# Gates and decoders of the experts: operands as two float32r parts with three products, and a second layer with early decay rates and one batch normalised by VectorE

## The reference, cut to what matters

```python
# one expert e; B = 4 batches of S = 512 tokens, D = 256 hidden features, 128 model features
mem = jnp.concatenate([hf, hb], axis=-1)                       # 512 features
gate_s = jax.nn.sigmoid(jax.nn.relu(mem @ sw1 + sb1) @ sw2 + sb2)
gate_t = jnp.tanh(jax.nn.relu(mem @ tw1 + tb1) @ tw2 + tb2)
g = gate_s * gate_t
out_e = _ln(jax.nn.relu(g @ dw1 + db1) @ dw2 + db2, dg, dbeta) # summed over e with the router's weights
...
# second layer: x = layer norm of the sum h
dt = sigmoid(x @ dt_w + dt_b) * 0.099 + 0.001
dA = exp(dt * -exp(A_log));  dBu = dt * (x @ B_mat.T)
hs[t] = dA[t] * hs[t - 1] + dBu[t]                             # over the 512 tokens of a batch
h = h + layer_norm(hs @ C_mat.T + D_vec * x) * gamma + beta
z = layer_norm(h)
out = h + (gelu(z @ tril(W1).T + b1) @ tril(W2).T + b2)        # over 128 features
```

## Time and profile before

| | |
|---|---|
| time, median of 3 runs | 5180.55 us (5178.99 to 5180.73) |
| the profiled execution: its own time | 5181.15 us |
| its span, first to last instruction | 5179.3 us |
| TensorE busy in the span | 5021.1 us, 97% |
| mean granted clock | 0.985 |
| the 16 steps on TensorE | 4695.4 us to about 5111 us |
| the second layer behind them | about 5111 us to 5179.3 us |

### The profile page before, as it was taken

How to read it: one execution, slowest core, us unless ns; L and a number is a source line. 1 busy time by engine, 2 the same in 40 slices (tenths; PEclk the granted TensorE clock), 3 DMA queues, 4 the chain that set the end, 5 groups by cost and what they waited for, 6 DMA issues and landing times. The chain is left out here.

```text
span 5179.3 us, 257985 instructions
## 1 busy us (share of the span) xinstructions
PE 5021.1 (97%) x108736; PEld 3531.4 (68%) x108736; DVE 4071.9 (79%) x19244; ACT 2374.2 (46%) x8355; POOL 1272.9 (25%) x5271
## 2 busy tenths in 40 slices
PE   7989799999999999999999999999999999998997
PEld 4656333333333337999999999999999999994444
DVE  3857666666666657999999999999999999992225
ACT  2734465555555543444444444444444444442334
POOL 0000032222221112333333333333333333330000
PEclk9989899999999999999999999999999999999998
DMA  0024644645544442110111011101111011102120
GB/s 15 1 89 155 144 100 120 137 119 127 122 114 106 97 167 91 25 41 17 41 25 41 17 41 25 41 21 37 41 25 41 18 41 25 41 1 91 50 69 10
DMA packets 393622, 327.33 MB, mean 63 GB/s; under 512 B 147001, under 2 KB 370745, under 8 KB 387546
## 3 DMA queue, kind: packets, MB, share of 16 engines
q1 hardware_dynamic: 393230, 323.37, 24.9%
HBM read 191.59 MB, written 131.60 MB: 62 GB/s over the span
## 5 line engine op out<-in xcount | busy, mean ns | idle before, releaser
L1475 PE MATMUL bank<-lparts,lstate 128*32 128x256 bf16 x98304 | 2698.6, 273 | 12.2 <-POOLq L1563 5.3
L1475 PEld LDWEIGHTS bank<-lparts,lstate 128*32 128x32 bf16 x98304 | 2460.9, 97 | 250.5 <-DVE lstate L1521 18.0
L1486 DVE STREAM_TRANSPOSE ltz<-bank 128x256 f32<-128x256 f32 x2048 | 922.2, 450 | 13.0 <-PE bank L1475 6.9
L1550 ACT ACTIVATE ltc<-lgc 128x16 f32<-128x16 f32 x2049 | 443.4, 216 | 1065.8 <-DVE lgc L1507 1065.8
L1584 POOL TENSOR_TENSOR lhs<-lgate,ltc 128x16 f32<-128x16 f32 x2052 | 474.3, 231 | 1756.2 <-ACT ltc L1550 1754.4
L1349 ACT ACTIVATE lparts<-bank 128x512 f32<-128x512 f32 x1024 | 549.9, 600 | 482.1 <-PE bank L1112 481.8
L1237 DVE TENSOR_REDUCE bnegmax<-bank 128x1 f32<-128x512 f32 x1024 | 654.5, 683 | 129.7 <-PE bank L1094 129.2
L1545 ACT ACTIVATE lgate<-lz 128x48 f32<-128x48 f32 x2048 | 498.8, 244 | 515.3 <-DVE lz L1497 515.2
L1493 DVE TENSOR_TENSOR lhalf<-ltz 128x128 f32<-128x128 f32 x2048 | 583.4, 285 | 4.1 <-issue 4.1
L1497 DVE TENSOR_TENSOR lz<-lhalf 128x64 f32<-128x64 f32 x2048 | 464.4, 227 | 0.6
L1300 POOL CAST bmaxparts<-bnegmax 128x4 bf16<-128x4 f32 x256 | 49.7, 194 | 1530.0 <-DVE bnegmax L1237 1530.0
(11 more groups left out here) (219 smaller groups left out, 4821.5 us busy)
## 6 DMA issues: line engine op xcount, KB each, us to landing
lparts<-qk SPq DMA_DIRECT2D x384, 128.0 KB, 6.2
zx<-lzsfirst SPq DMA_DIRECT2D x16, 2048.0 KB, 6.3
zx<-lzxsecond SPq DMA_DIRECT2D x16, 2048.0 KB, 7.3
lzxsecond<-zx SPq DMA_DIRECT2D x32, 1024.0 KB, 7.7
lzxfirst<-zx SPq DMA_DIRECT2D x30, 1024.0 KB, 7.4
qk<-eparts SPq DMA_DIRECT2D x96, 256.0 KB, 2.8
hs<-lhs SPq DMA_DIRECT2D x32, 512.0 KB, 5.8
cmemT<-hs SPq DMA_DIRECT2D x32, 512.0 KB, 4.8
```

The costliest lines, as they stand in the source:

```text
L1475: last = nc.tensor.matmul(bank[x][32 * q:32 * q + 32, 0:256], top[:, x, e, k].rearrange("p m r -> p (m r)"), parts[:, way, g, k, n, e, q], ...
L1486: nc.vector.transpose(tz[:, x].rearrange("p (n w) -> p n w", w=SLOT)[:, :, 0:32], bank[x][:, 0:256].rearrange("p (n c) -> p n c", n=BLOCKS ...
L1550: nc.scalar.activation(tc[:, x], gc[:, x, 1], ACT.Tanh).then_inc(tanhed[x], 1)
```

## The change

- Every operand of `hidden`, `gates` and `decode1` is written as two parts of type float32r: a high part (the value cast to float32r) and a low part (the value less the high part). A product of two float32 operands becomes three products of parts: high x high, high x low and low x high. `decode2` stays in float32.
- The weights are split in pieces of 512 columns: the sigmoid gate's first weights by VectorE, the others by GpSimd. The states of step 0 are split by ScalarE and VectorE, those of all other steps by GpSimd. ScalarE writes the hidden values twice (once as the high part, once in float32), and VectorE subtracts. VectorE also splits `g`.
- The raw weights `cw` and the raw states `cmemT` have one buffer instead of two, and so have the split weights `cwparts`; the split states `cmemparts` have two. The queue now loads states for step s once those of step s - 1 have been split. `cdw` holds the decoder's last weights in two buffers.
- The second layer's small loads are issued at the start, behind expert 1's weights, instead of behind the last states. `exp(A_log)` is computed in step 2 instead of behind step 15.
- `read_states(1)` stands ahead of `steps_and_inputs(3)`. VectorE normalises batch 2 of the last normalisation, ScalarE batch 3.
- Several tiles of the second layer share memory with tiles that are no longer needed.

```diff
+    HIGH, LOW = range(2)
+    PRODUCTS = ((HIGH, HIGH), (HIGH, LOW), (LOW, HIGH))
+    SPLIT_W = POST["dw2"]
+    SPLIT = 512
+    BESIDE = 2
...
-        w = core.sb(ctx, "cw", [P, 2, POST_W])
+        w = core.sb(ctx, "cw", [P, SPLIT_W])
+        parts = core.sb(ctx, "cwparts", [P, 2, SPLIT_W], F32R)
+        dw2 = core.sb(ctx, "cdw2", [P, 2, POST_W - SPLIT_W])
...
-        memT = core.sb(ctx, "cmemT", [P, 2, 4, S])
+        memT = core.sb(ctx, "cmemT", [P, 4, S])
+        mem_parts = core.sb(ctx, "cmemparts", [P, 2, 2, 4, S], F32R)
         hid = core.sb(ctx, "chid", [P, 4, S])
+        hid_parts = core.sb(ctx, "chidparts", [P, 2, 4, S], F32R)
...
+        g_parts = core.sb(ctx, "cgparts", [P, 2, KH, S], F32R)
...
+        sig, dt, da = (w[:, n * HALVES * S:(n + 1) * HALVES * S].rearrange("p (h s) -> p h s", h=HALVES) for n in range(3))
+        dbu, st = hid[:, 0:HALVES], hid[:, HALVES:2 * HALVES]
...
+        act_out, hb, result = memT, hbeta, sg
...
                 def load_states(s):
+                    if s > 0:
+                        sp.wait_ge(mem_low, 4 * s)
                     for way in range(2):
-                        sp.dma_start(memT[:, s % 2, 2 * way:2 * way + 2],
-                                     d["hs"][way, :, s // B, s % B].rearrange("k p t -> p k t")
-                                     ).then_inc(mem_in[s % 2], 16)
-                def load_weights(e, lo, hi, signal):
-                    sp.dma_start(w[:, e % 2, lo:hi], d["w_after"][e, :, lo:hi]).then_inc(signal[e % 2], 16)
+                        sp.dma_start(memT[:, 2 * way:2 * way + 2],
+                                     d["hs"][way, :, s // B, s % B].rearrange("k p t -> p k t")).then_inc(mem_in, 16)
+                def load_weights(e, lo, hi, signal, split, per_expert):
+                    if e > 0:
+                        sp.wait_ge(split, per_expert * e)
+                    sp.dma_start(w[:, lo:hi], d["w_after"][e, :, lo:hi]).then_inc(signal, 16)
...
+                    sp.dma_start(dw2[:, e % 2], d["w_after"][e, :, SPLIT_W:POST_W]).then_inc(dw2_in[e % 2], 16)
+                def load_first_weights(e):
+                    load_weights(e, 0, POST["tw1"], sw_in, sw_low, 2)
+                def load_later_weights(e):
+                    load_weights(e, POST["tw1"], POST["sw2"], tw_in, tw_low, 2)
+                    load_weights(e, POST["sw2"], SPLIT_W, rest_in, rest_low, 3)
+                load_first_weights(0)
                 load_states(0)
-                load_expert(0)
+                load_later_weights(0)
+                load_vectors(0)
+                load_vectors(1)
                 load_states(1)
-                load_expert(1)
+                load_first_weights(1)
+                load_later_weights(1)
+                load_tail()
                 for s in range(2, STEPS):
-                    sp.wait_ge(hid_mm, 4 * (s - 1))
                     load_states(s)
                     if s % B == 1 and 1 < s // B + 1 < E:
                         e = s // B + 1
                         sp.wait_ge(y_mm, B * (e - 1))
                         sp.wait_ge(summed, BT * B * (e - 1))
-                        load_expert(e)
-                load_tail()
+                        load_first_weights(e)
+                        load_later_weights(e)
+                        load_vectors(e)
...
+                def split_states(s):
+                    pool.wait_ge(mem_in, 32 * (s + 1))
+                    if s >= 2:
+                        pool.wait_ge(hid_mm, 4 * (s - 1))
+                    for k in range(4):
+                        high, low = (mem_parts[:, s % 2, part, k] for part in (HIGH, LOW))
+                        nc.gpsimd.tensor_copy(high, memT[:, k]).then_inc(mem_high, 1)
+                        pool.wait_ge(mem_high, 4 * s + k + 1)
+                        nc.gpsimd.tensor_tensor(low, memT[:, k], high, ALU.subtract).then_inc(mem_low, 1)
...
+                def split_hidden_weights(e):
+                    pool.wait_ge(tw_in, 16 * (e + 1))
+                    if e > 0:
+                        pool.wait_ge(hid_mm, 4 * B * e)
+                    for n in range(2):
+                        split_columns(POST["tw1"] + n * SPLIT, tw_high, tw_low, 2 * e + n + 1)
...
+                def split_decoder_weights(e):
+                    if e > 0:
+                        pool.wait_ge(d1_mm, KH * B * e)
+                    split_columns(POST["dw1"], rest_high, rest_low, 3 * e + 3)
+                split_hidden_weights(0)
+                split_gate_weights(0)
+                for s in range(1, STEPS):
+                    split_states(s)
+                    if s % B == 1:
+                        split_decoder_weights(s // B)
+                    elif s % B == 0:
+                        split_hidden_weights(s // B)
+                        split_gate_weights(s // B)
...
                         if s % B == 0 and m % 2 == 0:
-                            pe.wait_ge((sw_in, tw_in)[m // 2][s // B % 2], 16 * (s // B // 2 + 1))
+                            pe.wait_ge((sw_low, tw_low)[m // 2], 2 * (s // B + 1))
                         for k in range(4):
-                            last = nc.tensor.matmul(bank[4 + m][:], weight(s, ("sw1", "tw1")[m // 2], k, m % 2),
-                                                    memT[:, s % 2, k], start=k == 0, stop=k == 3)
+                            if m == 0:
+                                pe.wait_ge(mem_low, 4 * s + k + 1)
+                            for of_w, of_x in PRODUCTS:
+                                last = nc.tensor.matmul(
+                                    bank[4 + m][:], weight(("sw1", "tw1")[m // 2], of_w, k, m % 2),
+                                    mem_parts[:, s % 2, of_x, k], start=k == 0 and (of_w, of_x) == PRODUCTS[0],
+                                    stop=k == 3 and (of_w, of_x) == PRODUCTS[-1])
                         last.then_inc(hid_mm, 1)
...
-                            pe.wait_ge(hid_kept, 4 * s + m // 2 * 2 + k + 1)
...
+                            pe.wait_ge(hid_low, 4 * s + m // 2 * 2 + k + 1)
...
-                    pe.wait_ge(product, KH * (s + 1))
+                    pe.wait_ge(g_low, KH * (s + 1))
+                    if s % B == 0:
+                        pe.wait_ge(rest_low, 3 * (s // B) + 3)
...
+                    if s % B == 0:
+                        pe.wait_ge(dw2_in[s // B % 2], 16 * (s // B // 2 + 1))
...
                 turn(IN, 3)
-                read_states(0)
+                for b in range(2):
+                    read_states(b)
                 steps_and_inputs(3)
                 feed_through(3)
-                for b in range(1, B):
+                for b in range(2, B):
                     read_states(b)
...
                     for m in range(4):
+                        bias = col(s, ("sb1", "tb1")[m // 2], m % 2)
                         act.wait_ge(hid_mm, 4 * s + m + 1)
-                        nc.scalar.activation(hid[:, m], bank[4 + m][:], ACT.Relu,
-                                             bias=col(s, ("sb1", "tb1")[m // 2], m % 2)).then_inc(hid_kept, 1)
+                        nc.scalar.activation(hid_parts[:, HIGH, m], bank[4 + m][:], ACT.Relu, bias=bias
+                                             ).then_inc(hid_high, 1)
+                        if s > 0:
+                            act.wait_ge(hid_low, 4 * (s - 1) + m + 1)
+                        nc.scalar.activation(hid[:, m], bank[4 + m][:], ACT.Relu, bias=bias).then_inc(hid_kept, 1)
...
+                    if s == 2:
+                        act.wait_ge(tail_in, TAIL_LOADS * 16)
+                        nc.scalar.activation(a[:], alog[:], ACT.Exp).then_inc(a_exp, 1)
...
-                act.wait_ge(tail_in, TAIL_LOADS * 16)
                 sigmoid(0)
-                nc.scalar.activation(a[:], alog[:], ACT.Exp).then_inc(a_exp, 1)
                 root_of(IN, 3)
...
-                for b in (2, 3):
-                    normalise(b)
-                    keep_turned(OUT, b)
+                normalise(3)
+                keep_turned(OUT, 2)
+                keep_turned(OUT, 3)
...
+                def split_first_weights(e):
+                    dve.wait_ge(sw_in, 16 * (e + 1))
+                    if e > 0:
+                        dve.wait_ge(hid_mm, 4 * B * e - 2)
+                    for n in range(2):
+                        at = POST["sw1"] + n * SPLIT
+                        high, low = (parts[:, part, at:at + SPLIT] for part in (HIGH, LOW))
+                        nc.vector.tensor_copy(high, w[:, at:at + SPLIT]).then_inc(sw_high, 1)
+                        dve.wait_ge(sw_high, 2 * e + n + 1)
+                        nc.vector.tensor_tensor(low, w[:, at:at + SPLIT], high, ALU.subtract).then_inc(sw_low, 1)
+                def rest_of_hidden(s, m):
+                    dve.wait_ge(hid_high, 4 * s + m + 1)
+                    dve.wait_ge(hid_kept, 4 * s + m + 1)
```

(31 more changed lines are left out.)

83 lines of the change are left out of this document (52 added, 31 removed).

## The result

The changed kernel takes 5126.26 us (median of 4 runs, 5125.63 to 5126.86), the kernel before in the same series 5180.59. The ratio is 0.9896, 95% interval 0.9879 to 0.9913: 54 us faster. I had forecast 5099, 82 us faster; the range (5082 to 5128) held the time.

What follows compares the result with a forecast made beforehand. TensorE's step was taken to bound the expert phase. 5181.15 - 94.4 (products) + 14.8 (stalls) + 1.4 (start) - 3.5 (second layer) = 5099.5, median 5099 us; own range 5088 to 5112, 8 in 10 5082 to 5128.

Steps and rivals of the forecast that it cites:

- rivals 2 to 4: VectorE late, 5123 us (9%); no stall in steps 6 and 10, 5084 (14%); GpSimd's casts dearer than 0.61 us, 5110 (10%).
- 512 columns ... I take one pass, 0.2133 + 0.0027 = 0.216 us: TensorE's expert steps: each float32r product takes one pass, making a step 19.92 us; -94.4 us over 16 steps.
- +1.4 us: Start of the expert phase: ScalarE's copy and VectorE's subtraction, 0.7 us each, come before the first product.
- Nothing, with next to no slack: Step 2: its states, behind other loads and GpSimd's splits, are ready at 4732 us, before `hidden(2)` at about 4734; no cost.
- so: nothing: VectorE in each expert step: its added casts and subtractions fit with some 3 us of slack; no cost.
- rival 2: Expert steps: VectorE becomes late beside GpSimd's work, 3 us in half the steps, +24 us, 5123 us; 9%.
- 7.4 us, twice: Steps 6 and 10: TensorE stalls for states queued behind the next expert's weights and then split by GpSimd; +14.8 us.
- Rival 3: Steps 6 and 10: no stall, as half the states' bytes may pass ahead of the weights; 5084 us, 14%.
- -3.5 us: Second layer: reordered work and a moved exponential save time, less a later VectorE entry; between -6 and +2.
- (a): Second layer: without `exp(A_log)` there, ScalarE saves a table load and 0.2 us before the first scan; -1.5 us.
- (b): Second layer: VectorE's statistics of batch 1 follow batch 0's at once, bringing the second scan earlier; -2.7 us.
- Rival 1: All three product blocks: a product costs more than a pass, making the kernel slower, about 5234 or 5371 us; 7%.

Runs made afterwards that it cites:

- experiment 1: The changed kernel with the parts of weights, states, hidden values and gates in bf16 instead of float32r; 5108.69 us.
- x_shapes: The changed kernel with the hidden layer's products cut into instructions of 128 columns and the gates' into 256, the decoder's left at 512; 5292.92 us.
- Experiment 5: The changed kernel with ScalarE's four copies of step 0's states ahead of its wait for the vectors instead of behind it; 5124.13 us.
- x_loads: The changed kernel with the weights of experts 2 and 3 issued one step later, behind the states of steps 6 and 10; 5112.13 us.
- x_read: The changed kernel with read_states of batch 1 back behind steps_and_inputs(3) and the feed-through; 5126.47 us.

## Why the prediction was right in sign and 27 us short

The time lies outside the forecast's own range (5088 to 5112) and 2 us inside the wide one, which rivals 2 to 4 had stretched; that it still fell inside is in part luck, as the last item below shows. By the prediction's own sign (wrong "if a product is not 0.21 to 0.22 us") the forecast failed, and so did another sign, "no wait of line 1905 on `chidparts`", of which there are 4.1 us. What held is the mechanism (three products of one pass each in place of four passes, in a step that TensorE bounds) and the stalls of steps 6 and 10, in place and in size.

By spans the change brought 55.4 us; my sum said 81.7. The 26.3 us between them, in the order of the prediction's steps:

- **"512 columns ... I take one pass, 0.2133 + 0.0027 = 0.216 us"**: the term that was mis-sized. It is 0.229; 1332 products up to `decode2(14)` (444 times three) at 13.2 ns are 17.5 us. I took the price of the bf16 row for a type that no row showed, and experiment 1 shows that the bf16 price is right for bf16 alone. The error of 6% in the price is 19% of the gain, because the gain is a difference (0.859 less three products).
- **"I add nothing" for the weight load** holds for the limit that I had in mind: 0.111 us is below a product, and x_shapes meets it, 0.1114, only at 128 columns. Whether part of the 13 ns is the load's is open, since experiment 1 changed both operands.
- **The start, "+1.4 us"**: 5.4, so 4.0 missing. I followed the states and the weights and left out what stood ahead of the copies in ScalarE's own row, the wait for the vectors, whose loads are issued behind all of expert 0's weights. Experiment 5.
- **"Nothing, with next to no slack" for step 2**: 2.7 us. The queue was named, but two of its terms were wrong. "GpSimd's nine pairs ... from about 4696.5, to 4714" ran on end in my count. In the changed kernel GpSimd first waited for the states of step 1, which the one raw buffer lets in only when those of step 0 are split (issued at 4702.93):

```profile
4708.68 1.06 POOL L1819 CAST cmemparts<-cmemT 128x512 fp32r<-128x512 f32 x1 [6.32 <-DMA cmemT<-hs]
...
4734.58 0.61 POOL L1819 CAST cmemparts<-cmemT 128x512 fp32r<-128x512 f32 x1 [14.37 <-DMA cmemT<-hs]
```

So the decoder split ended at 4720.2, and the states of step 2 were issued at 4726.3 instead of 4719.5. Their landing then took 7.7 us instead of 4.8. `hidden(2)` began at 4739.0 and not at 4734, which hid part of it.

- **VectorE, "so: nothing"**: failed; rival 2 in its place. I took 3 us of slack from rows of operations that ran alone; beside GpSimd they take up to 1.8 us. It cost 5.1 us, in steps 4, 8 and 12 only, and not in half the steps. The Trainium skill's sentence, cited at rival 2 ("GPSIMD Engine Reference", section Key points), names two kinds of VectorE instructions that GpSimd contends with, those with two SBUF inputs and those in a 2-port perf mode. With the first kind `cyg` above agrees: 1.81 against 0.69 us. `cyn`, with one tensor input, is slower there too, 3.43 us for four, where the same four take 1.11 us alone; whether it is of the second kind no row here tells.
- **Steps 6 and 10, "7.4 us, twice"**: 8.1 and 7.2. Right in place, releaser and size. Rival 3 fell.
- **The second layer, "-3.5 us"**: -6.3, with the last `decode1`'s 0.7 left out. Alone the parts are worth 2.4, 0.4 and 0.3 us of the stretch (the last two within its scatter), where I had 1.5, 2.7 and 0.8, and together 7.2: what I missed is that either (a) or (b) is enough to take the slow clock behind the first scan off the path. I had written (b) as 14.3 to 11.7 us between the scans; it is 9.7.
- Not in my sum: 1.3 us more in step 0, 1.1 of them by the slow clock in the first `hidden` (0.50 until 4704 us), and -2.1 us from ahead of the phase, where nothing was edited. That last part is luck, not the change: between two profiles of the changed kernel alone it moves by 5 us.

Together 17.5 + 4.0 + 2.7 + 5.1 + 0.5 - 2.8 + 1.3 - 2.1 = 26.2, all but 0.1. Rival 1 (a price near 0.277 or above) did not come; its mechanism did, at a fifth of that distance.

## What to carry to other kernels

A gain that is a difference of two prices magnifies an error of either: give a type that no row shows its own range, and multiply it out. When a change turns idle engines into helpers, take no duration from rows in which they ran alone, and read every wait that stands ahead of a new instruction in its engine's own order, also the ones that the change didn't touch. In one queue, a load that is wanted soon belongs ahead of a load whose issue has to wait for another engine; moving one `if` by a step was worth 14 us.

## What the runs showed of the hardware that I had not expected

- A float32r product of 512 columns takes 0.229 us where a bf16 one takes 0.216, 256 columns 0.118, 128 columns 0.111.
- A VectorE subtraction or product of 512 columns takes 0.69 us alone, and `cyg` took 1.81 beside GpSimd; four one-input operations of 128 columns took 3.43 us instead of 1.11.
- In step 4 two stops of TensorE, 1.4 and 0.7 us, were followed by a granted clock of 0.50 in one trace (x_loads) and of 1.00 in another (changed), with the same code in this stage; the slow one adds 1.6 us. In step 2 of x_read it added 2.7.
- Edits in the last 70 us left the stages ahead alone, yet the expert phase began up to 10 us earlier or later. The changed kernel itself did so from one profile to the next (4685.06 and 4690.14).
